# Embedding tower on one core: lookups moved ahead of the products, another order of stages, fewer gather rows and a fourth one-hot chunk

## The reference

```python
e = jnp.stack([tbl_0[ids[:, 0]], ..., tbl_25[ids[:, 25]]], axis=1)
combined = jnp.concatenate([dense_features[:, None, :], e], axis=1)   # (B, 27, 128)
interactions = jnp.einsum('bfd,bgd->bfg', combined, combined)
z = jnp.concatenate([dense_features, interactions[:, _TRIU_I, _TRIU_J]], axis=1)
h = jnp.concatenate([z, dense_features], axis=1)
h = jnp.maximum(h @ W_top1 + b_top1, 0.0)       # 607 -> 512
h = jnp.maximum(h @ W_top2 + b_top2, 0.0)       # 512 -> 256
y = h @ W_top3                                  # 256 -> 1
```

## Time and profile of the kernel before

| what | us |
|---|---|
| median of 3 runs | 520.17 |
| lowest and highest run | 515.14, 522.7 |
| the profiled execution | 515.3 |
| its span | 513.2 |
| PE, DVE, ACT, POOL busy (share of the span) | 408.8 (80%), 262.7 (51%), 208.7 (41%), 254.1 (50%) |
| moved by DMA | 36.34 MB, 71 GB/s |
| mean granted clock of PE | 0.88 |

### The profile page before, as it was taken

How to read it: one execution, slowest core, us unless ns; L and a number is a source line. 1 busy time by engine, 2 the same in 40 slices (tenths; PEclk the granted TensorE clock), 3 DMA queues, 4 the chain that set the end, 5 groups by cost and what they waited for, 6 DMA issues and landing times.

```text
span 513.2 us, 14192 instructions
## 1 busy us (share of the span) xinstructions
PE 408.8 (80%) x6280; PEld 365.9 (71%) x6280; DVE 262.7 (51%) x323; ACT 208.7 (41%) x436; POOL 254.1 (50%) x265
## 2 busy tenths in 40 slices
PE   5886727777978598875978788887989689789977
PEld 4776716767878497764967687785878588778755
DVE  3789505654555554663553655655364655454220
ACT  3456302234343543444342553435243543337432
POOL 5778875551555555552555535553555535540000
PEclk8998857776999898988897978997898969899989
DMA  6994251230322222221222212221232212210000
GB/s 170 227 240 107 67 158 50 70 108 23 74 59 78 56 64 68 69 64 32 64 66 70 63 49 64 67 74 49 68 68 69 63 42 70 58 39 1 4 1 0
DMA packets 27972, 36.34 MB, mean 71 GB/s; under 512 B 9151, under 2 KB 21959, under 8 KB 27912
## 3 DMA queue, kind: packets, MB, share of 16 engines
q1 hardware_dynamic: 19704, 18.65, 14.6%
q0 software_dynamic: 8192, 16.79, 13.5%
q10 hardware_dynamic: 16, 0.01, 0.0%
HBM read 35.42 MB, written 0.01 MB: 69 GB/s over the span
## 4 chain that ended last, share of the span: by engine, by line
PE 71%; issue 13%; ACT 4%; SPq 4%; DMA 4%; DVE 2%; another core or an unknown queue 1%; ACTq 0%; DVEq 0%
PE ring L411 17%; PE ring L412 15%; PE gram L449 10%; PE ring L485 8%; PE ring L431 7%; PE ring L494 6%; DMA dense<-in_r_dense_features 4%; PE ring L483 3%; SPq L281 2%; PE ring L461 2%; PE ring L472 2%; DVE pairs_and_more L674 2%; PE ring L503 2%; ACT pairs_and_more L578 1%; SPq L275 1%
## 5 line engine op out<-in xcount | busy, mean ns | idle before, releaser
L359 POOL DMA_INDIRECT rows<-in_tbl,ids_all x256 | 248.7, 971 | 201.1 <-PE gram L449 127.3
L651 DVE TENSOR_TENSOR onehot<-idb,vrow 125x1024 fp32r<-125x1024 f32 x160 | 192.7, 1222 | 130.5 <-PE ring L412 58.7
L411 PE MATMUL ring<-onehot,table_hi 125*128 125x256 f32 x608 | 181.6, 328 | 22.1 <-DVE pairs_and_more L674 7.6
L412 PE MATMUL ring<-onehot,table_lo 125*128 125x256 f32 x608 | 169.5, 309 | 0.0
L411 PEld LDWEIGHTS ring<-onehot,table_hi 125*128 125x128 f32 x608 | 132.9, 219 | 28.8 <-issue 8.7
L412 PEld LDWEIGHTS ring<-onehot,table_lo 125*128 125x128 f32 x608 | 133.4, 219 | 0.8
L559 ACT COPY xt<-ring 128x256 f32<-128x256 f32 x80 | 54.2, 677 | 128.9 <-PE ring L412 68.3
L449 PE MATMUL gram<-xt 128*27 128x26 f32 x4096 | 55.1, 201 | 42.6 <-issue 40.0
L449 PEld LDWEIGHTS gram<-xt 128*27 128x27 f32 x4096 | 47.8, 114 | 51.7 <-issue 46.0
L567 ACT COPY xt<-ring 128x512 f32<-128x512 f32 (+1 forms) x56 | 51.2, 987 | 24.1 <-remote 16.0
L431 PE MATMUL ring<-ident,rows 128*128 128x128 f32 x256 | 38.6, 285 | 13.6 <-issue 6.7
(11 more groups left out here) (41 smaller groups left out, 209.7 us busy)
## 6 DMA issues: line engine op xcount, KB each, us to landing
ids_spread<-in_ids_t SPq DMA_DIRECT2D x70, 128.0 KB
rows<-in_tbl,ids_all POOLq DMA_INDIRECT x256
xt<-in_tbl SPq DMA_DIRECT2D x6, 448.0 KB
w<-in_tbl SPq DMA_DIRECT2D x3, 448.0 KB
rows<-in_ids_t SPq DMA_DIRECT2D x10, 128.0 KB, 5.7
dense<-in_r_dense_features SPq DMA_DIRECT2D x16, 64.0 KB
w<-in_W_top SPq DMA_DIRECT2D x4, 256.0 KB
w<-in_W_top SPq DMA_DIRECT2D x1, 512.0 KB
```

The costliest lines, as they stand in the source:

```text
L359: pool.indirect_dma_start(rows[:, i % ROWS, :], None, aps[f"tbl_{f}"], bass.IndirectOffsetOnAxis(ap=ids_all[:, k, f:f + 1].bitcast(U32), a ...
L411: pe.matmul(ps, table_hi[:, m, c * KC + k, :], chosen, start=first, stop=False)
L412: last = pe.matmul(ps, table_lo[:, m, c * KC + k, :], chosen, start=False, stop=final)
L651: dve.tensor_tensor(onehot[:, (CH * u + c) % SLOTS], idb[0:VP, u % 2, 0:BS].unsqueeze(1).to_broadcast([VP, KC, BS]), vrow[:, c * KC:(c + 1 ...
```

## The change

- `ROWS` 45 to 37, `SLOTS` 3 to 4 (two whole lookups of one-hots).
- The ids of the first ten lookups no longer come by ten broadcasts. One DMA of 10 KB brings them, ACT casts them, and PE spreads each row over the partitions with a matmul against a column of the identity, straight into `idb` (new stage `first_ids`). `ids_t` holds only the ten columns used.
- The two dense tiles are loaded between the tables and no longer behind them; all five rows banks of the first tile stand together ahead of lookup 9.
- `stages()` is another list: three lookups of batch n+2 stand in the last quarter of batch n, so that many more lookups are done when the product steps of a batch begin; unblock, rows and pairs stand at the head of a quarter, lookups at its end; unblock and pairs of batch n-1 have moved into the quarters of batch n. The copy of a product step has a stage of its own, `grams`, steps 0 and 2 on DVE, 1 and 3 on ACT; step 0's copy waits until `unblock` of the batch before has read `A`.
- `layer1` is 2 uses of the ring with two blocks each (before: 4 with one), `pairs` 2 uses (before: 3).
- DVE makes the one-hots two lookups ahead in one piece (`one_hot(u + 1, 0, 1)` behind `lower_part(u)`), ACT casts ids three ahead.
- Rows banks on DVE: 1 and 3 of the second tile (before: 1 of both tiles and 3 of the second).
- A group of gathers waits for `gram_ready, group - 3`, one product step later; group 4 is no longer behind a lookup. POOL does its two lower parts ahead of group 3, before: behind group 3.

```diff
-ROWS = 45
+ROWS = 37
...
-    SLOTS = 3
+    SLOTS = 4
...
         for n in range(NB):
             yield "products", n, 0, 0
+            yield from layer("unblock", n - 1, 0, 1)
+            yield from lookups(n + 1, *([0, 1, 2] if n == 0 else [3]))
+            yield from layer("unblock", n - 1, 2, 3)
+            yield "grams", n, 0, 0
+            yield from layer("layer3", n - 2, 0)
+            yield from rows(n, 1, 0, 1)
+            yield from lookups(n + 1, *([3] if n == 0 else [4, 5]))
+
+            yield "products", n, 1, 0
+            yield "grams", n, 1, 0
+            yield from layer("pairs", n - 1, 0, 1)
+            yield from lookups(n + 1, *([4, 5] if n == 0 else [6]))
+            yield from rows(n, 1, 2, 3, 4)
             yield from layer("layer1", n - 1, 0)
+            yield from lookups(n + 1, *([6] if n == 0 else [7]))
+
+            yield "products", n, 2, 0
+            yield "grams", n, 2, 0
             yield from layer("layer1", n - 1, 1)
...
+            yield from lookups(n + 1, *([7] if n == 0 else []))
+            yield from rows(n + 1, 0, 0, 1)
+            yield from lookups(n + 1, 8, 9)
+
+            yield "products", n, 3, 0
+            yield "grams", n, 3, 0
+            yield from layer("layer2", n - 1, 0)
+            yield from rows(n + 1, 0, 2, 3, 4)
+            yield from lookups(n + 2, 0)
             if n == NB - 1:
...
+                yield from layer("unblock", n, 0, 1)
             yield from layer("layer2", n - 1, 1)
...
+            yield from lookups(n + 2, 1, 2)
+        yield from layer("unblock", NB - 1, 2, 3)
+        yield from layer("layer3", NB - 2, 0)
+        yield from layer("pairs", NB - 1, 0, 1)
+        yield from layer("layer1", NB - 1, 0, 1)
...
-    FIRST_GROUPS_BEHIND = {1: 0, 2: 3, 3: 6, 4: 9}
+    FIRST_GROUPS_BEHIND = {1: 0, 2: 3, 3: 6}
...
-                    pool.wait_ge(gram_ready, group - 4)
+                    pool.wait_ge(gram_ready, group - 3)
...
                     i = k * NG + g
+                    if (k, g) == (1, GROUP):
+                        for m in LO_ON_GPSIMD:
+                            lower_part(m)
...
+            def spread_first_ids(m):
+                if m == 0:
+
+                    pe.wait_ge(first_ids_ready, 1)
+                if m >= 2:
+
+                    pe.wait_ge(onehot_ready, CH * (m - 1))
+                pe.matmul(idb[0:VP, m % 2, 0:BS], ident[0:NL, m:m + 1].to_broadcast([NL, VP]), first_ids, start=True,
+                          stop=True).then_inc(first_idb_ready, 1)
...
                 dve.wait_ge(gram_ready, n * STEPS + s + 1)
+                if s == 0 and n > 0:
+
+                    dve.wait_ge(ring_filled, filled("unblock", n - 1, NU - 1, 0))
                 dve.tensor_copy(*product_views(s)).then_inc(gram_dve, 1)
...
             one_hot(0, 0, 1)
+            one_hot(1, 0, 1)
             for stage, n, a, b in stages():
                 if stage == "lookup":
                     u = n * NL + a + 1
-                    if u < NB * NL:
-                        one_hot(u, 0)
-                        if u < NL and u not in FROM_RAW:
-                            lower_part(u)
-                        elif u >= NL and u - NL in FROM_RAW[:2]:
-                            lower_part(u - NL)
-                        one_hot(u, 1)
+                    if u < NL and u not in FROM_RAW:
+                        lower_part(u)
+                    elif u >= NL and u - NL in FROM_RAW[:2]:
+                        lower_part(u - NL)
+                    if u + 1 < NB * NL:
+                        one_hot(u + 1, 0, 1)
```

More of the change, by code:

```diff
@@ L81, in layer @@
                     yield stage, n, b, 0
[L83 to L86, removed]
+        yield "first_ids", 0, 0, 0
+        yield "first_ids", 0, 1, 0
+        for m in range(NL - 1):
+            if m + 2 < NL:
+                yield "first_ids", 0, m + 2, 0
+            yield from lookups(0, m)
+        yield from rows(0, 0, 0, 1, 2, 3, 4)
         yield from lookups(0, NL - 1)
@@ L193, in build @@
         y_row = beside_pairs[:, 0:BS]
[L195 to L203, removed]
+        first_ids_i = pairs_and_more[0:NL, 0, 0:BS].bitcast(I32)
+        first_ids = pairs_and_more[0:NL, 1, 0:BS]
         W = KT * D
@@ L218, in build @@
         ids_landed = sem("ids_landed")
-        first_ids_landed = [sem(f"first_ids_landed{m}") for m in range(NL)]
+        first_ids_landed = sem("first_ids_landed")
+        first_ids_ready = sem("first_ids_ready")
+        first_idb_ready = sem("first_idb_ready")
         ids_spread_landed = [sem(f"ids_spread_landed{q}") for q in range(IDS_SLOTS)]
@@ L510, in _ @@
             for stage, n, a, b in stages():
-                if stage == "lookup":
+                if stage == "first_ids":
+                    spread_first_ids(a)
+                elif stage == "lookup":
                     lookup(n, a)
@@ L579, in store_unblocked, with store_pairs, store_layer1, store_layer2 @@
                 last.then_inc(left("unblock", n, b, 0), 1)
-            def store_pairs(n, k):
-                w = K_PAIR[k][1]
-                ps = bank("pairs", n, k, 0)
-                act.copy(x[0:w, k, :], ps[0:w, 0:BS]).then_inc(left("pairs", n, k, 0), 1)
-            def store_layer(stage, n, b, h_next, bias):
-                ps = bank(stage, n, b, 0)
-                act.activation(h_next[:, b, :], ps[:, 0:BS], ACT.Relu, bias=bias[:, b:b + 1]).then_inc(left(stage, n, b, 0), 1)
+            def store_pairs(n, b):
+                ps = bank("pairs", n, b, 0)
+                k, w = (slice(0, 2), P) if b == 0 else (slice(2, 3), K_PAIR[2][1])
+                act.copy(x[0:w, k, :].rearrange("p k s -> p (k s)"), ps[0:w, 0:(k.stop - k.start) * BS]).then_inc(
+                    left("pairs", n, b, 0), 1)
+            def store_layer1(n, b):
+                ps = bank("layer1", n, b, 0)
+                for i in range(2):
+                    block = 2 * b + i
+                    last = act.activation(h1[:, block, :], ps[:, i * BS:(i + 1) * BS], ACT.Relu, bias=b1[:, block:block + 1])
+                last.then_inc(left("layer1", n, b, 0), 1)
+            def store_layer2(n, b):
+                ps = bank("layer2", n, b, 0)
+                act.activation(h2[:, b, :], ps[:, 0:BS], ACT.Relu, bias=b2[:, b:b + 1]).then_inc(left("layer2", n, b, 0), 1)
             def store_y(n):
@@ L616, in _ @@
                     store_rows(n, a, b)
-                elif stage == "products" and a % 2 == 0:
+                elif stage == "grams" and a % 2 == 1:
                     store_products(n, a)
@@ L699, in _ @@
                     store_unblocked(n, a)
-                elif stage == "products" and a % 2 == 1:
+                elif stage == "grams" and a % 2 == 0:
                     store_products(n, a)
```

126 lines of the change are left out of this document (43 added, 83 removed).

## The result

The changed kernel takes 475.15 us (median of 4 runs, 473.75 to 480.61) against 518.75 of the kernel before on the same chip (4 runs, 515.14 to 522.7): ratio 0.921, 95% interval 0.9154 to 0.9267. It is 8% faster. The profiled execution takes 474.73 us with a span of 472.9. Medians in this document are over all runs; ratios and intervals compare only the runs in the faster of two states in which executions come, so a ratio can differ a little from that of the medians.

A forecast was written before the change was run, and what follows sets the result against it. POOL's gathers were taken to hold PE, at least 12.9 us a quarter. 57.5 + 4 x 12.9 + 6 x 52.5 + 46, plus 2.5 and 2.1, gave 474.7, put at 477 us; range 458 to 502.

The forecast's parts named there:

- The order: Batch stages: awaited work moves to quarter heads, away from late events; second and fourth quarters fall from 13.85 and 17.43 us.
- The floor: Quarters with gathers: start 0.3, eight gathers 9.7, wait 1.6, rest of product step 1.28; at least 12.9 us.
- the 1.6 us: Product steps: PE runs freely only about 1.6 us after POOL's last gather, read as gathers holding PE.
- the floor isn't one: Rival, chance 0.07: POOL and PE only coincide, quarters go to PE's work, 10.5 to 11.8 us; total 407.
- The first quarter, 13.8: Batches 1 to 6: DVE's queue delays unblock bank 3 and lookups 4 and 5; 13.8 us, bounds 12.9 and 15.4.
- The fourth quarter, 12.9: Last quarter of a batch: PE's work of 11.8 us lies under 12.9, so it takes 12.9.
- PE no longer meets a one-hot that waits for a late event: Lookups, one-hots made further ahead: nothing gained below 12.9 us a quarter; 1.22 us per chunk if the cover fails.
- The start, 57.5: End of product step 0: PE there at about 45, held by POOL's gathers until 57.5 us; bounds 45.5 and 60.
- the spreads: Start: PE's small matmuls spreading ids cost about 0.3 us each, hidden by the tables' arrival.
- The tail, 46: After product step 0 of batch 7: unblock and pairs move in, 41.42 us become 46, bounds 43 and 49.
- The sum: Whole kernel: start, 28 quarters and tail give 470.1, plus 2.5 excess 472.6 us of span; execution 474.7, put at 477.
- The ports: SBUF: the skill says TensorE and ScalarE never wait on anyone, so whatever couples PE and ACT to POOL isn't that port.

The follow-up runs named there:

- Experiment 9: The changed kernel with the earlier order of stages inside the batches, on a chip where gathers hold PE: 504.68 us, ratio 0.9805 to the kernel before.
- experiment 7: The changed kernel with gathers from the fourth tile on replaced by plain 64 KB DMAs issued by SP: 399.51 us, kernel before 519.41.
- experiment 11: The changed kernel with gathers from the fourth tile on replaced by plain 64 KB DMAs issued by POOL: 399.56 us, kernel before 516.74.
- experiment 6: The changed kernel, unchanged, against the kernel before on another chip where gathers hold PE: 476.28 us, ratio 0.929.
- experiment 10: The changed kernel with layer 3 and a lookup earlier, unblock bank 3 on ACT, POOL's lower parts behind the second tile's gathers: 482.95 us, kernel before 516.74.
- experiment 4: The changed kernel with the earlier order of stages inside the batches, on a chip where gathers don't hold PE: 415.95 us, ratio 1.0249 to the kernel before.

## Why the prediction was right, and where only its sum was

**The order.** Right, with its mechanism: late events no longer meet work that others wait for. Experiment 9 took the order back and got the old quarters. The predicted 477 stands beside 475.15, the span of 472.6 beside 472.9.

**The floor.** Right on the chips that have it, from batch 1 on: 12.9 in the second and third quarters (means 12.97 and 12.91 of six). I called the 1.6 us the sign that POOL's gathers are what holds PE, from coincidence alone; experiment 7 shows that they do, and experiment 11 that it isn't the number or size of the packets. I also gave 0.07 to "the floor isn't one", with 407. On one chip of those used it isn't one, and that time would have been about right there: the kernel with plain DMAs, nearest to the changed one, took 391. How the changed kernel itself compares with the 406 of that chip was not measured. The case I had not thought of is that both hold, on different chips.

**The first quarter, 13.8.** Confirmed step by step. DVE behind the product step that ends at 270.78:

```profile
269.85 3.48 DVE L664 TENSOR_TENSOR onehot<-idb,vrow 125x1024 fp32r<-125x1024 f32 x3
273.24 1.42 DVE L690 COPY pairs_and_more<-ring 64x80 f32<-64x80 f32 x6
274.69 2.36 DVE L664 TENSOR_TENSOR onehot<-idb,vrow 125x1024 fp32r<-125x1024 f32 x2
276.97 1.48 DVE L690 COPY pairs_and_more<-ring 64x32 f32<-64x32 f32 x8
...
278.50 0.39 PE L413 MATMUL ring<-onehot,table_hi 125*128 125x256 f32 x1 [1.65 <-issue]
```

Bank 1 is stored 3.9 us after the step (4.1 predicted), the one-hots by 6.3 (6.5), bank 3 by 7.7 (8.0), and lookup 4, which reuses its bank, starts in the same moment. Five of the six first quarters take 13.24 to 13.98, the sixth 15.73, above the bound of 15.4; mean 14.05.

**The fourth quarter, 12.9.** Mis-sized: 12.74 to 13.86, mean 13.35. The step that failed is "PE no longer meets a one-hot that waits for a late event". DVE in the fourth quarter of batch 3:

```profile
262.88 1.23 DVE L664 TENSOR_TENSOR onehot<-idb,vrow 125x1024 fp32r<-125x1024 f32 x1 [4.67 <-PE ring L414]
267.08 1.23 DVE L664 TENSOR_TENSOR onehot<-idb,vrow 125x1024 fp32r<-125x1024 f32 x1 [2.97 <-PE ring L414]
```

The second chunk waits for the end of a lookup that PE left at 263.42 and hears of it at 267.08, 3.7 us late; the last lookup of the quarter waits for that chunk until 268.36. In three of the six fourth quarters this costs 0.9. Two lookups ahead is not always enough.

**The start, 57.5.** The number is right (57.90), the working isn't. PE was to be at step 0 by 45, to be held for 12 us, and to be let go 1.6 us after POOL's fourth group. PE, and POOL's last gather of that group:

```profile
54.86 0.57 PE L451 MATMUL gram<-xt 128*27 128x26 f32 x44 [1.05 <-ACT xt L562]
...
57.06 0.84 PE L451 MATMUL gram<-xt 128*27 128x26 f32 x75 [0.50 <-issue]
...
55.38 0.95 POOL L354 DMA_INDIRECT rows<-in_tbl,ids_all  x1 [0.30 <-issue]
```

PE came at 54.86. The group ended at 56.33 (54 predicted), and the last 75 matmuls start 0.73 us later, not 1.6; by the rule the step would have ended at 56.33 + 1.6 + 1.3 = 59.2. In the changed kernel's trace of experiment 6, where that group ends at 56.56, the step isn't held at all:

```profile
56.52 1.27 PE L451 MATMUL gram<-xt 128*27 128x26 f32 x128 [1.05 <-ACT xt L562]
```

The same start runs in experiments 7, 9 and 11, where step 0 also takes 1.27 us and ends at 57.5 to 57.6. What set the end of step 0 was PE's own late arrival, in the first trace with 1.8 us of standing in the step, and not the floor; that both come to 57.5 is luck.

Why PE was late is known in part. The arrival of the tables was to hide the spreads, at 0.3 each; but from 10 to 40 us PE is busy 29.09 of 30 us (25.24 before), and a spread costs 0.62 (the lookup behind the one at 15.95 starts at 16.57). No run shows the 0.3. Then there is a wait, DVE beside POOL:

```profile
39.26 5.70 DVE L650 TENSOR_TENSOR table_lo<-xt,table_hi 125x1024 fp32r<-125x1024 f32 x1
...
39.18 4.69 POOL L331 TENSOR_TENSOR table_lo<-w,table_hi 125x1024 fp32r<-125x1024 f32 x2
```

A lower part on DVE, 1.22 us by itself, takes 5.70 beside POOL's two lower parts, and ends 1.1 us after them; lookup 8 waits for it, 4.25 us. POOL isn't slowed (4.71 in the earlier trace rows). I had moved POOL's lower parts in thought without asking what DVE does in the same 5 us. The Trainium skill (SBUF — State Buffer, "SBUF: two separate sides") has this case: DVE operations with two SBUF inputs and GpSimd operations that read SBUF lock each other out for the whole instruction. These rows agree with it, and so do experiments 6 and 9, where the same part begins later, takes 4.82 and 3.27, and again ends 1.1 us after POOL's. But it isn't the whole delay: in experiment 10, where no lower part of DVE takes over 1.22, PE still comes to step 0 only at 54.30.

**The tail, 46.** Mis-sized: 41.6. The added work is there, PE busy 37.22 us against 33.98, but the 2 us of new waits aren't, and old ones went: PE idles 4.4 us in place of 7.4.

**The sum.** Start + 0.4, quarters + 4.3 (373.4 against 28 x 13.18), tail - 4.4. Of the quarters' excess the fourth ones make 2.7, batch 0 2.1 and the first ones 1.5, less most of the 2.5 that the sum had put on top. That the hit is so close is luck twice: quarters and tail cancel, and the start came right for another reason. What is no luck is the mechanism that makes the change faster, late events that no longer meet work that others wait for.

**The ports.** The sentence of the Trainium skill (SBUF — State Buffer, "SBUF: two separate sides") quoted ahead, that TensorE and ScalarE have their own SBUF ports and never wait on anyone, isn't contradicted: experiment 7 shows the coupling to be with POOL's indirect issuing, and nothing shows it to be at a port. What the path is stays open.

## What to carry to other kernels

When a busy engine shows gaps of "issue" that nothing explains, lay the other engines' timelines beside it and measure the distance from their last instruction to its restart: a constant distance, here 1.6 us, names the partner. While POOL issues indirect gathers, put work whose results nobody awaits beside them, keep the runs short (the order bears eight; 16 took 164 us more, in part for another reason), start them only when PE's burst is over, and place what others wait for ahead of them. And compare on more than one chip: the same kernel took 406 and 518 us, and a change that is worth 8% on one kind needn't be worth that on the other (its part without the order gained 2% with the hold and lost 2.5% without it).

## What the runs showed of the hardware that was not expected

- On the chip of the first comparison and on three of the four used later PE can't issue freely during POOL's indirect gathers and its semaphore events arrive late, up to 8 us. On the fourth, in experiment 4, the three steps within its run of 40 gathers take 1.9, 1.9 and 2.4 us, with one stand of 0.4, and neither ACT nor DVE stands until 1.6 us after a run. The kernel before takes 509 to 525 us on the former and 402 to 409 on the latter.
- The hold depends on when the gathers begin: if 0.27 us after a product step, they leave the head of a quarter prompt; if in it (1.03 us after its start, at about its 100th matmul), nearly every event waits until 1.7 us after their end. Mean quarters: 13.3 and 20.7 us. In the start, at steps 0 and 1, the hold ends sooner (0.73 and 1.23 us after the gathers) or isn't there.
- In runs of 16 gathers a lookup goes down to one matmul in 1.4 us from 10.6 us into the run on.
- 256 short matmuls back to back stand for 0.6 to 3.1 us with no gather running, each time until 2.2 to 2.9 us after the start of a 16 KB packet of PE's instruction queue.
- Plain DMAs of the same 64 KB cost POOL 0.53 us each (4.23 for eight), and no hold was seen beside them; indirect ones are 1.25 us apart (9.7 for eight).
- A DVE subtraction of two SBUF operands took 5.70, 4.82 and 3.27 us beside POOL's, each time ending 1.1 us after them, and 1.22 alone.
